# Triangle attention and triangle multiplication: four-bank sums, a new run-out, and all constants added by TensorE

## The chip, the cores and the metric

The kernel runs on one core of a Trainium2 chip. The metric is the device time of one execution in microseconds, the median of several runs; for the kernel before it is 250.66 us (three runs, 250.49 to 250.67).

## The reference

`x` is a map of 96 x 96 tokens with 32 channels. Two residual layers follow each other, each on a group norm `_gn` of its input with one channel to a group (mean and variance over all 9216 tokens).

```python
x = x + L0(_gn(x));  x = x + L1(_gn(x))
# L0: triangle attention, 4 heads of 32, one softmax row per (i, q, head)
xn = layernorm(x) * ln_gamma + ln_beta
scores = einsum('biqhd,biKhd->bihqK', q, k) + tri_bias + mask_bias
o = einsum('bihqk,bikhd->biqhd', softmax(scores), v) * sigmoid(xn @ wg + bg)
out = o @ wo + bo
# L1: triangle multiplication
zn = layernorm(z) * ln_in_w + ln_in_b
a = mask * sigmoid(zn @ a_g + ..) * (zn @ a_p + ..);  b likewise
t = einsum('bikh,bjkh->bijh', a, b)
out = sigmoid(zn @ g_w + g_b) * ((layernorm(t) * ln_out_w + ln_out_b) @ z_w + z_b)
```

All of it is float32.

## The kernel before, in words

Rows of the map are taken in 24 blocks of four rows, and six quads of four blocks. Every engine has its own program, and semaphores tie them; the order of each engine's work is written out by hand, and each engine works its list off in that order. PSUM has eight banks of 512 float32 columns, which the stages share.

**Attention loop.** 72 tiles of 128 queries, in 36 pairs. `step_pe`, `step_act`, `step_dve`, `step_pool` write out step k of each engine, 40 steps in all. ScalarE takes the exponentials of pair k (`exponentials`, L763); VectorE inverts the sums (L1119); GpSimd multiplies pair k-1 by them (L572); TensorE turns pair k-2 into banks 2 and 3 (L1418); VectorE copies both banks (L1131); TensorE multiplies pair k-3 with the values into bank 1 (L1432). A finished block g of four rows is gated by VectorE (`o_group`, L1140), projected by TensorE (`y_group`, L1443) into the same bank 1, and added to the residual (L1145), which releases `y_added`. The run-out is steps 35 to 39, in which no new pair comes in. In it TensorE also turns residual quads 0 to 3 (`res_transposes`, L1220), which ScalarE copies (`res_copy`, L646).

**Second norm** (`norm_front(1)`). VectorE sums what `y_added` released, ScalarE takes squares of the last blocks (L778), a matmul spreads the statistic (L1240), residual quads 4 and 5 are turned behind it, and 24 matmuls center the quads (L1263; two records each). ScalarE squares them (L680), VectorE sums the squares over channels (L964) in two parts of three quads, ScalarE takes the root (L697), VectorE scales (L973), TensorE turns the normalized quads (L1291) and ScalarE copies them (L702). `idle_products` are matmuls whose result nobody reads; the list `IDLE` says how many stand at each place.

**Projection loop.** Eight sets of three blocks: TensorE projects (L1473, L1478), VectorE multiplies one part by the mask (L1165), ScalarE takes sigmoids (L834 for a and b, L836 for the output gate), VectorE multiplies (L1175). GpSimd meanwhile prepares quads 0 and 1: gate times z constant, added to the residual (L616, L618, `CONST_SETS`).

**Tail.** 32 products per channel fill all eight banks (L1497). VectorE subtracts a pivot into SBUF (L1045), ScalarE squares (L842), GpSimd adds squares (L598). VectorE adds the eight banks up (`add_scores`, L1034, L1032; each releases its bank through `sums_read`), makes the variance, and ScalarE the root (L849). TensorE turns the maps (L1523), multiplies by the z weights (`z_products`, L1508), and for quads 2 to 5 adds the z constant times the deviation (`z_constant`, L1515). Quads 0 and 1 are gated by VectorE before the root (L1014), scaled by ScalarE in 32 pieces (L858), and added to the residual by GpSimd (L456). Quads 2 to 5 have their gates scaled first (L450, by VectorE for quad 2, by GpSimd for 3 to 5), and then VectorE gates and adds. The twelve stores (L436) go out in three batches of two quads each: `FIRST`, `SECOND`, `EARLY`, issued from the queues of SP and ScalarE, each behind a wait for `out_ready` or `out_more`.

## Time and profile before

| | |
|---|---|
| median of three runs | 250.66 us |
| the profiled execution, its own time | 250.1 us |
| its span, first to last instruction | 248.3 us |
| mean granted TensorE clock | 0.969 |
| TensorE busy | 213.9 us (86%) |
| VectorE busy | 184.7 us (74%) |
| ScalarE busy | 188.2 us (76%) |
| GpSimd busy | 110.1 us (44%) |
| output stores | 12 of 96.0 KB, eight issued by SP, four by ScalarE |

The span is shorter than the execution's own time by 1.8 us, which lie ahead of the first and behind the last instruction. Engines are named as in the page of the profile: PE is TensorE (PEld its weight loads), DVE VectorE, ACT ScalarE, POOL GpSimd, SP the queue of SyncE. A float32 matmul may leave two records. A timeline row gives the start and the length of a piece, and in brackets how long the engine stood before it and what ended that.

### The profile page before, as it was taken

How to read it: one execution, taken by the hardware profiler on the slowest of the kernel's cores; microseconds unless marked ns; L12 is line 12 of the kernel's file. 1: busy time of each engine (PE TensorE's matmuls, PEld its weight loads, DVE VectorE, ACT ScalarE, POOL GpSimd, SP SyncE). 2: the span in 40 equal slices, each digit the busy share in tenths (PEclk: the TensorE clock that was granted, in tenths of full speed). 3: DMA queues.
4: the chain of work that ended last, by engine and by line, in shares of the span. 5: the costliest groups of instructions: out<-in, count | busy, mean ns of one | idle time of the engine just before them, and what ended most of it. 6: DMA issues, size and time to landing. Idle time of an engine off the chain costs nothing. (4 is left out here: it accounts for less than half of the span.)

```text
span 248.3 us, 6918 instructions
## 1 busy us (share of the span) xinstructions
PE 213.9 (86%) x2492; PEld 184.7 (74%) x2492; DVE 184.7 (74%) x356; ACT 188.2 (76%) x792; POOL 110.1 (44%) x110
## 2 busy tenths in 40 slices
PE   6979984789999999999999999999879875697830
PEld 6969733678889889888888889888758764596510
DVE  6755867446878787787888797787658859979890
ACT  0765982799988999899989989999855865676380
POOL 2100001067575765857675675844500328036281
PEclk9997999799999999999999999999999999999985
DMA  8500035665454646454464644330000000000038
GB/s 128 90 13 15 8 127 168 238 238 181 166 199 151 243 150 215 154 194 167 164 226 141 235 162 154 130 134 3 0 3 3 0 3 0 4 0 3 0 65 127
DMA packets 42992, 27.30 MB, mean 110 GB/s; under 512 B 24976, under 2 KB 42942, under 8 KB 42958
## 3 DMA queue, kind: packets, MB, share of 16 engines
q1 hardware_dynamic: 38614, 26.27, 33.1%
q10 hardware_dynamic: 4216, 0.51, 1.5%
q8 instruction: 20, 0.33, 0.5%
q0 software_dynamic: 128, 0.08, 0.2%
q14 instruction: 14, 0.11, 0.1%
HBM read 1.36 MB, written 1.18 MB: 10 GB/s over the span
## 5 line engine op out<-in xcount | busy, mean ns | idle before, releaser
L763 ACT ACTIVATE maps<-psum,neg_max 128x96 f32<-128x96 f32 x288 | 94.8, 356 | 10.5 <-PE psum L1418 7.2
L572 POOL TENSOR_TENSOR maps<-maps,rden 128x768 f32<-128x768 f32 x36 | 53.0, 1472 | 43.9 <-DVE rden L1119 43.9
L763 ACT ACTIVATION_READ_ACCUMULATOR maps<-psum,neg_max 128x1 f32 x288 | 63.8, 221 | 0.0
L1109 DVE TENSOR_REDUCE neg_max<-psum 128x8 f32<-128x768 f32 x36 | 34.5, 958 | 28.4 <-PE psum L1392 28.4
L1131 DVE COPY turned<-psum 96x1024 f32<-96x1024 f32 x36 | 43.6, 1212 | 5.2 <-PE psum L1418 3.8
L1418 PE MATMUL psum<-ident,maps 128*96 128x128 f32 x288 | 37.5, 273 | 1.6 <-DVE turned L1131 0.8
L1418 PEld LDWEIGHTS psum<-ident,maps 128*96 128x96 f32 x288 | 31.6, 126 | 3.1 <-DVE turned L1131 1.1
L1385 PE MATMUL psum<-u_st,x_stack 128*128 128x384 f32 x72 | 25.7, 358 | 2.1 <-DMA u_st<-u_split 2.1
L1191 PE MATMUL psum<-tri_b,ones_r 128*96 128x192 f32 x187 | 23.0, 278 | 2.6 <-DVE ones_r L888 2.2
L1387 PE MATMUL psum<-u_st,x_stack 128*96 128x384 f32 x72 | 24.8, 345 | 0.0
L1392 PE MATMUL psum<-bias_lo,token_ident 100*128 100x384 f32 x72 | 24.8, 344 | 0.0
L1390 PE MATMUL psum<-bias_hi,token_ident 96*128 96x384 f32 x72 | 24.8, 344 | 0.0
L1432 PE MATMUL psum<-turned,maps 128*32 128x96 f32 x768 | 23.3, 250 | 1.1 <-DVE shared L1145 1.1
L1191 PEld LDWEIGHTS psum<-tri_b,ones_r 128*96 128x96 f32 x187 | 20.4, 182 | 3.5 <-DVE ones_r L888 2.2
L581 POOL TENSOR_TENSOR u_split<-u_full,u_split 128x384 fp32r<-128x384 f32 x21 | 21.2, 1008 | 1.7
L1432 PEld LDWEIGHTS psum<-turned,maps 128*32 128x32 f32 x768 | 15.6, 109 | 7.7 <-issue 6.4
L806 ACT ACTIVATE g_sb<-psum,bg_half 128x384 f32<-128x384 f32 x24 | 14.4, 600 | 2.9 <-PE psum L1364 2.9
L1385 PEld LDWEIGHTS psum<-u_st,x_stack 128*128 128x128 f32 x72 | 13.9, 193 | 2.5 <-issue 2.5
L579 POOL CAST u_split<-u_full 128x384 fp32r<-128x384 f32 x21 | 10.6, 506 | 11.4 <-DVE u_full L1125 11.4
L1390 PEld LDWEIGHTS psum<-bias_hi,token_ident 96*128 96x128 f32 x72 | 13.8, 192 | 1.2
L772 ACT ACTIVATE maps<-psum 96x512 f32<-96x512 f32 x24 | 14.4, 602 | 0.0
L1374 PEld LDWEIGHTS psum<-wv_st,x_stack 128*96 128x96 f32 x96 | 10.9, 164 | 4.7 <-DVE u_full L1125 4.2
(199 smaller groups left out, 417.5 us busy)
## 6 DMA issues: line engine op xcount, KB each, us to landing
u_st<-u_split SPq DMA_DIRECT2D x96, 192.0 KB
x_stack<-shared SPq DMA_DIRECT2D x40, 96.0 KB, 2.0
maps<-in_x SPq DMA_DIRECT2D x8, 144.0 KB, 3.5
out_y<-maps SPq DMA_DIRECT2D x8, 96.0 KB, 2.3
x_stack<-shared SPq DMA_DIRECT2D x4, 144.0 KB, 2.1
bias_lo<-gate_sb SPq DMA_DIRECT2D x24, 18.0 KB
out_y<-maps ACTq DMA_DIRECT2D x4, 96.0 KB, 3.7
x_stack<-shared SPq DMA_DIRECT2D x4, 48.0 KB, 1.9
```

The lines of the kernel that those rows point to most:

```text
L572: pool.tensor_tensor(at, at, rden[:, rows, :].unsqueeze(3).to_broadcast([P, 2, H, N]), ALU.mult).then_inc(probs_ready, 1)
L581: pool.tensor_tensor(u_split[:, g % U_SLOTS, 1], u_full[:, :], u_split[:, g % U_SLOTS, 0].bitcast(f32), ALU.subtract).then_inc(u_lo, 1)
L763: e = act.activation(probs[:, t // 2 % SLOTS, t % 2, h], bank_s[t % 4][:, h * N:(h + 1) * N], ACT.Exp, bias=neg_max[:, t % BODY, h:h + 1], ...
L1109: dve.tensor_reduce(neg_max[:, rows_of(k), :], scores.rearrange("p r (h k) -> p r h k", h=H), AX.X, ALU.max, negate=True).then_inc(max_rea ...
L1131: dve.tensor_copy(turned[0:N, :, 2 * (j % SPAN):2 * (j % SPAN) + 2].rearrange("p h n t -> p n h t"), psum[0:N, 2 * BANK:4 * BANK].rearrang ...
L1191: pe.matmul(banks[bank][0:N, 0:PW + C], ones_r[:, :], tri_b[:, 0:PW + C], start=True, stop=True)
L1385: pe.matmul(bank_s[t % 4][:, 0:H * N], x_columns[:, last - N:last + P - N], u_st[:, g % STAGES, :, GROUP - 1, :], start=True, stop=False)
L1387: pe.matmul(bank_s[t % 4][0:N, 0:H * N], x_stack[:, i, g, :], u_st[:, g % STAGES, :, i, :], start=True, stop=False, skip_group_check=True)
L1390: pe.matmul(scores, token_ident[0:N, i], bias_hi[0:N].rearrange("p h k -> p (h k)"), start=False, stop=False)
L1392: pe.matmul(scores, token_ident[0:MASK_ROWS, i], bias_lo[0:MASK_ROWS, g % STAGES, i].rearrange("p h k -> p (h k)"), start=False, stop=True ...
L1418: mm = pe.transpose(bank_t[n][0:N, h * P:(h + 1) * P], probs[:, j % SLOTS, n, h, :], ident[:, :])
L1432: mm = pe.matmul(bank_o[h * C:(h + 1) * C, i * N:(i + 1) * N], values[:, g % V_SLOTS, i, h * C:(h + 1) * C], probs_t, start=True, stop=True)
```

## The change

Four places are touched.

- *Run-out.* GpSimd multiplies only the first tile of the last pair, VectorE the second. The last pair is turned into banks 4 and 5 instead of 2 and 3, in the same step as the pair before it. The last block's output goes to bank 3 instead of bank 1. The last gate is projected one step earlier. Residual quads 0 to 2 (instead of 0 to 3) are turned in steps 37 and 38, and ScalarE copies them after the loop; 3 to 5 follow behind the statistic matmul. Six idle products before the last projection go.
- *Second norm.* For the last three quads GpSimd adds the two halves of the 32 squares first, and VectorE sums 16. Ten idle products become two.
- *Projection loop.* GpSimd's preparation of quads 0 and 1 goes; TensorE adds the constants of all six quads.
- *Tail.* The sums over eight banks become two reductions over four banks each. GpSimd adds all the squares and folds them. No quad is gated ahead of the root. The gates of quad 0 are scaled by VectorE, of 1 to 3 by GpSimd, of 4 and 5 by ScalarE in 32 pieces; GpSimd adds the residual of quads 1 and 3, VectorE of the others. The stores go out in the order of the quads.

```diff
--- before.py
+++ after.py
@@ constants @@
-POOL_QUADS = 2
-FIRST, SECOND, EARLY = (2, 3), (4, 5), (0, 1)
+POOL_SCALES, ACT_SCALES, POOL_ADDS = (1, 2, 3), (4, 5), (1, 3)
...
 def gate_group(k):
+            if k >= PAIRS:
+                return BLOCKS - 1 if k == PAIRS else None
...
-        RES_EARLY = 4
-        RES_BANKS = 4
+        RES_EARLY = 3
         def res_bank(q):
-            return 4 + q % RES_BANKS
+            return (6, 7, 4, 5, 7, 4)[q]
+        def turning_bank(j):
+            return 4 if j == PAIRS - 1 else 2
+        def turned_at(k):
+            if k >= PAIRS:
+                return (PAIRS - 2, PAIRS - 1) if k == PAIRS else ()
+            return (k - T_BEHIND,) if live(k - T_BEHIND) else ()
+        def out_bank(g):
+            return banks[3] if g == BLOCKS - 1 else bank_o
...
-        IDLE = (32, 6, 8, 4, 2, 3, 6, 10, 24)
+        IDLE = (32, 6, 8, 4, 2, 3, 6, 2, 24)
@@ sync: the stores @@
-            for quads, rows in ((FIRST, range(GROUP)), (SECOND, range(2)), (EARLY, range(2))):
-                if quads[0]:
-                    sp.wait_ge(out_ready, quads[-1] + 1 - POOL_QUADS)
-                else:
-                    sp.wait_ge(out_more, POOL_QUADS)
+            for quads, rows, ready, more in (((0, 1), range(GROUP), 1, 1), ((2, 3), range(2), 2, 2), ((4, 5), range(2), 4, 2)):
+                sp.wait_ge(out_ready, ready)
+                sp.wait_ge(out_more, more)
@@ gpsimd @@
                 if live(k - 1):
+                    tiles = 1 if k == PAIRS else 2
+                    at = probs[:, (k - 1) % SLOTS, 0:tiles]
...
+            for q in parts(1)[1]:
+                at = slice(4 * q, 4 * q + 4)
+                pool.wait_ge(d_squared, QUADS + q + 1)
+                pool.tensor_tensor(work[:, at, :, 0:C // 2], work[:, at, :, 0:C // 2], work[:, at, :, C // 2:C],
+                                   ALU.add).then_inc(d_folded, 1)
...
-                for n in range(1, TRI_BANKS - 1):
+                for n in range(1, TRI_BANKS):
...
+                pool.wait_ge(squares_added, TRI_BANKS - 1)
+                pool.tensor_tensor(square_parts[:, :, 0:2], square_parts[:, :, 0:2], square_parts[:, :, 2:4],
+                                   ALU.add).then_inc(squares_added, 1)
+                pool.wait_ge(squares_added, TRI_BANKS)
+                pool.tensor_tensor(moments[:, 2], square_parts[:, :, 0], square_parts[:, :, 1],
+                                   ALU.add).then_inc(squares_added, 1)
...
-                for q in range(POOL_QUADS + 1, QUADS):
+                for q in POOL_SCALES:
                     scale_gates(pool, q).then_inc(gates_scaled, 1)
-                for q in range(POOL_QUADS):
-                    pool.wait_ge(scaled_more, q + 1)
+                for n, q in enumerate(POOL_ADDS):
+                    pool.wait_ge(z_gated, n + 1)
                     add_residual(pool, q).then_inc(out_more, 1)
-            for n in range(CONST_SETS):
...
-                pool.wait_ge(gates_ready, 2 * n + 2)
-                pool.tensor_tensor(product, gate_sb[:, at], constant, ALU.mult).then_inc(const_gated, 1)
-                pool.tensor_tensor(res[:, at], res[:, at], product, ALU.add).then_inc(const_gated, 1)
@@ scalar @@
-                for q in (2 * (k - PAIRS), 2 * (k - PAIRS) + 1):
-                    if 0 <= q < RES_EARLY:
-                        res_copy(q)
...
             load_table(2, ACT.Sqrt)
+            res_copy(0)
+            res_copy(1)
             square_outputs(QUADS - 1, slice(BLOCKS - 4, BLOCKS - 1))
             square_outputs(QUADS, slice(BLOCKS - 1, BLOCKS))
+            res_copy(2)
...
-            for q in range(POOL_QUADS):
-                act.wait_ge(z_gated, q + 1)
+            for q in ACT_SCALES:
                 for b in range(4 * q, 4 * q + 4):
                     for f in range(GROUP):
-                        scaled = act.activation(square[:, b, f], square[:, b, f], ACT.Copy, scale=inverse[:, b, f:f + 1])
+                        scaled = act.activation(gate_sb[:, b, f], gate_sb[:, b, f], ACT.Copy, scale=inverse[:, b, f:f + 1])
...
@@ vector @@
+                        if layer and part:
+                            dve.wait_ge(d_folded, q + 1 - QUADS // 2)
+                            members_of = slice(0, C // 2)
...
+                        ins = dve.tensor_reduce(tok[:, 0, at], work[:, at, :, members_of], AX.X, ALU.add)
...
+                def total_of(n):
+                    four = psum[0:N, 4 * n * BANK:4 * (n + 1) * BANK].rearrange("j (k x) -> j k x", k=4)[:, :, 0:GN]
+                    dve.tensor_reduce(halves[:, n], four.rearrange("j k (h f b) -> j b f k h", h=GROUP, f=GROUP), AX.XY,
+                                      ALU.add).then_inc(sums_read, 1)
...
-                for n in range(TRI_BANKS):
-                    add_scores(n)
+                for n in range(2):
+                    total_of(n)
...
-                for q in range(POOL_QUADS):
-                    gate_z(q).then_inc(z_gated, 1)
                 dve.wait_ge(root_ready, 6)
...
+                if k == PAIRS - 1:
+                    dve.wait_ge(exp_done, TILES - 1)
+                    dve.reciprocal(rden[:, last.start, :], den[:, last.start, :]).then_inc(rden_ready, 1)
...
+                if k == PAIRS - 1:
+                    dve.wait_ge(exp_done, TILES)
+                    dve.reciprocal(rden[:, last.stop - 1, :], den[:, last.stop - 1, :]).then_inc(rden_ready, 1)
+                    at = probs[:, (PAIRS - 1) % SLOTS, 1]
+                    dve.wait_ge(rden_ready, PAIRS + 1)
+                    dve.tensor_tensor(at, at, rden[:, last.stop - 1, :].unsqueeze(2).to_broadcast([P, H, N]),
+                                      ALU.mult).then_inc(last_scaled, 1)
...
-                if y is not None:
+                if y is not None and g != BLOCKS - 1:
                     dve.wait_ge(y_done, y + 1)
...
-            link(scale_gates(dve, POOL_QUADS))
-            for q in range(POOL_QUADS, QUADS):
-                need(dve, gates_scaled, q - POOL_QUADS)
-                link(gate_z(q))
-                add_residual(dve, q).then_inc(out_ready, 1)
+            link(scale_gates(dve, 0))
+            for q in range(QUADS):
+                if q in POOL_SCALES:
+                    dve.wait_ge(gates_scaled, POOL_SCALES.index(q) + 1)
+                elif q in ACT_SCALES:
+                    dve.wait_ge(scaled_more, ACT_SCALES.index(q) + 1)
+                if q in POOL_ADDS:
+                    gate_z(q).then_inc(z_gated, 1)
+                else:
+                    link(gate_z(q))
+                    add_residual(dve, q).then_inc(out_ready, 1)
@@ tensor @@
+                for j in turned_at(k):
...
+                        pe.wait_ge(exp_done, TILES)
+                        pe.wait_ge(probs_ready, PAIRS)
+                        pe.wait_ge(last_scaled, 1)
...
+                if k == PAIRS + 1:
+                    res_transposes(0)
...
-                        idle_products(IDLE_BANKS[0], IDLE[6])
...
+                if PAIRS < k < STEPS - 1:
+                    res_transposes(k - PAIRS)
...
-                    pe.wait_ge(sums_read, GROUP + q + 1)
+                    pe.wait_ge(sums_read, 2)
...
-                if q < GROUP:
-                    pe.wait_ge(sums_read, q + 1)
+                if not q:
+                    pe.wait_ge(sums_read, 1)
...
-            for q in (2, 3, 4):
+            for q in range(5):
                 z_constant(q)
```

## Rows read from the trace of the kernel before

**Rows 1.** Chain of waits, in order of time: start, length (us), what.

```profile
185.42 0.34 DVE shared L1145 x2
...
198.68 1.07 PE psum L1191 x10
...
224.66 0.48 DVE turned L1034
```

**Rows 2.** Timeline of GpSimd, run-out: start, length (us), line, operation, [idle before].

```profile
174.78 1.47 POOL L572 TENSOR_TENSOR maps<-maps,rden 128x768 f32<-128x768 f32 x1 [0.69 <-DVE rden L1119]
177.53 1.47 POOL L572 TENSOR_TENSOR maps<-maps,rden 128x768 f32<-128x768 f32 x1 [1.28 <-DVE rden L1119]
```

**Rows 3.** Timeline of TensorE, run-out.

```profile
179.78 1.08 PE L1418 MATMUL psum<-ident,maps 128*96 128x128 f32 x8 [0.85 <-DVE turned L1131]
```

**Rows 4.** Timeline of VectorE, run-out.

```profile
175.42 1.22 DVE L1131 COPY turned<-psum 96x1024 f32<-96x1024 f32 x1 [0.72 <-PE psum L1418]
...
180.90 1.22 DVE L1131 COPY turned<-psum 96x1024 f32<-96x1024 f32 x1 [1.17 <-PE psum L1418]
```

**Rows 5.** Timeline of TensorE, second norm.

```profile
186.80 1.05 PE L1220 MATMUL psum<-ident,shared 128*96 128x128 f32 x8
...
188.39 5.48 PE L1263 MATMUL psum<-centering_r,shared 128*96 128x128 f32 x48 [0.18 <-DVE centering_r L952]
```

**Rows 6.** Windows, projection loop: stretch, its length, busy us by engine, clock, DMA.

```profile
203.00:218.40 15.40, 10.37 (x208) 8.31 (x201) 14.67 (x15) 9.26 (x16) 6.95 (x6) 1.00 0.01 3
```

**Rows 7.** Line L1175, durations ns min/median/max.

```profile
L1175 DVE TENSOR_TENSOR shared<-maps,turned x6: 942/1058/1664, 204.5 to 217.3; 96x768 f32<-96x768 f32 x6
```

**Rows 8.** Timeline of all engines, start of the projection loop.

```profile
204.33 0.99 POOL L618 TENSOR_TENSOR res_memory<-res_memory,u_split 96x384 f32<-96x384 f32 x1
204.47 1.66 DVE L1175 TENSOR_TENSOR shared<-maps,turned 96x768 f32<-96x768 f32 x1
```

**Rows 9.** Timeline of ScalarE, second norm.

```profile
195.27 1.99 ACT L702 ACTIVATE shared<-psum,w_all 128x384 f32<-128x384 f32 x3
197.52 0.24 ACT L697 ACTIVATE tok<-tok 96x48 f32<-96x48 f32 x1 [0.27 <-DVE tok L981]
```

**Rows 10.** Lines L1109 and L992, the reductions: durations ns min/median/max.

```profile
L1109 DVE TENSOR_REDUCE neg_max<-psum x36: 957/958/959, 45.7 to 171.5; 128x8 f32<-128x768 f32 x36
...
L992 DVE TENSOR_REDUCE u_split<-ident x1: 249/249/249, 190.4 to 190.4; 96x32 f32<-96x96 f32 x1
```

**Rows 11.** Timeline of TensorE, tail.

```profile
225.27 2.87 PE L1523 MATMUL psum<-ident,maps 96*128 96x96 f32 x24 [1.20 <-DVE turned L1034]
227.98 3.66 PE L1508 MATMUL psum<-g_sb,shared 128*96 128x128 f32 x32
...
233.72 1.95 PE L1515 MATMUL psum<-u_split 32*96 32x512 f32 x6
```

**Rows 12.** Timelines of GpSimd and ScalarE, tail.

```profile
222.50 5.57 POOL L598 TENSOR_TENSOR turned<-turned,maps 96x384 f32<-96x384 f32 x5
...
241.12 1.75 POOL L456 TENSOR_TENSOR maps<-maps,res_memory 96x512 f32<-96x512 f32 x1 [1.24 <-ACT maps L858]
...
234.15 6.89 ACT L858 ACTIVATE maps<-maps,tok 96x32 f32<-96x32 f32 x32 [0.95 <-DVE tok L1063]
```

**Rows 13.** Timeline of VectorE, tail.

```profile
235.28 0.69 DVE L1014 TENSOR_TENSOR maps<-psum,gate_sb 96x512 f32<-96x512 f32 x1 [0.44 <-DVE gate_sb L450]
236.00 1.30 DVE L456 TENSOR_TENSOR maps<-maps,res_memory 96x512 f32<-96x512 f32 x1
...
241.06 0.69 DVE L456 TENSOR_TENSOR maps<-maps,res_memory 96x512 f32<-96x512 f32 x1
```

**Rows 14.** Windows, stores: DMA share and GB/s are the last two columns.

```profile
244.00:246.00 2.00, 0.00 (x0) 0.00 (x0) 0.00 (x0) 0.00 (x0) 0.00 (x0) 0.50 1.30 189
```

**Rows 15.** Windows, first norm: the granted clock is the third column from the end.

```profile
14.00:16.00 2.00, 1.05 (x8) 0.84 (x8) 0.68 (x1) 1.57 (x2) 0.00 (x0) 1.00 0.01 1
...
18.00:20.00 2.00, 2.00 (x11) 2.00 (x10) 0.87 (x2) 0.59 (x1) 0.00 (x0) 0.50 0.08 20
```

111 lines of the change are left out of this document (49 added, 62 removed).

## The prediction

> **What bounds the kernel now.** First the chain of waits read in order of time [rows 1]: TensorE, VectorE and ScalarE hand one thread to each other, and no engine is the limit everywhere. So each stretch the diff touches is read in its timelines, for the wait that ends last there.
>
> *Run-out of the attention loop, to 185.76 us.* GpSimd normalizes the last pair of tiles from 177.53 to 179.00 [rows 2]; TensorE turns it only at 179.78, having waited for VectorE to copy the pair before out of the same two banks [rows 3]; VectorE copies it at 180.90 [rows 4], and the run-out ends with the last residual add at 185.76 [rows 1].
>
> *Second norm, 185.8 to 203.6.* Behind the statistic matmul stand the transposes of two residual quads; on the chain then 5.48 us of centering [rows 5], and later ten idle products, 1.07 us, ahead of the fourth group of transposes [rows 1].
>
> *Projection loop, 203.6 to 218.3.* VectorE is busy 14.67 of 15.40 us, GpSimd 6.95 [rows 6]. One of VectorE's products lasts 1.66 us, the quickest of that line 0.94 [rows 7].
>
> *Tail, 218.4 to 248.3.* VectorE adds eight banks one by one, TensorE makes the z products, root and gates follow, and the twelve stores end it.
>
> **The change part by part.** Times are on the clock of the profiled run before (span 248.3 us, 250.1 us in all, so 1.8 around it; 0.56 below the median 250.66). The sum is taken off the median.
>
> *Run-out.* The pair 34 leaves GpSimd at 174.78 + 1.47 = 176.25 [rows 2]. Of pair 35 GpSimd now takes the first tile only, 384 elements, about 1.0 us by a 384-element row (0.99, [rows 8]): to 177.27. VectorE takes the second, after copying pair 33 (175.4 + 1.2 = 176.6, some 0.2 earlier without the residual transposes ahead of it [rows 4]) and a short reciprocal. This product reads two tensors from SBUF, as GpSimd's does. Such a meeting is in [rows 8]: VectorE's product starts at 204.47 while GpSimd runs until 205.32 and takes 1.66, which is 0.85 of waiting and 0.81 of work; so VectorE stands until 177.27 and ends near 177.8.
>
> The Trainium skill, "SBUF — State Buffer", section "Who interferes with whom", makes a rule of it: VectorE with two SBUF inputs and GpSimd exclude each other for a whole instruction, while VectorE with one SBUF input is free. The trace agrees in the waiting of 0.85 us above; by sharing in place of waiting the run-out would gain some 0.4 more.
>
> TensorE turns pair 35 at 177.9 into banks 4 and 5, with no wait for VectorE (179.78 before). VectorE's queue then decides: output 21 and residual 20 (0.75), the copy of 34 to 179.75, the copy of 35 to 180.9, against 180.90 + 1.22 = 182.12: 1.2 us. The rest of the gain is order: the last value products write bank 3, so they wait for output 22 alone (181.4), not for the residual add behind it; the last output is formed ahead of residual 22; six idle products go. Chain: 181.4, value products 0.9, output 0.5, y 0.4, add 0.45: 183.7. Gain 2.05. Costed at nothing: the new wait for the last exponentials, with output 21 queued behind it on VectorE, since ScalarE is done with them before the copy of 33 ends at 176.6; the last gate's projection, a step earlier behind a wait for output 21, since only residual quad 0 queues behind it; ScalarE's table load and two residual copies ahead of the squares, done by 182.4, where the squares can start at 183.0. Uncovered, each would cost its own half to one us once. But a third residual quad now stands behind the statistic matmul: four more transposes at 0.81/8 each are 0.41, of which 0.18 us of TensorE's idle time ahead of centering hides a part [rows 5]. **Term: -1.8** (bounds -2.5 with sharing and a hidden quad, -1.0 if the order gains nothing).
>
> *Second norm.* GpSimd halves the squares of three quads (96x256 each; 0.7 to 1.4 us by its products of 0.99 for 384 elements, slowed or not [rows 8]) and has been idle there, so VectorE's three sums of 512 become 256, saving 3 x 256 x 1.04 ns = 0.8 us. But ScalarE is busy with three copies from 195.27 to 197.26 and takes the root at 197.52 [rows 9], so only 0.25 reaches the root. The idle products 10 to 2 are worth more: eight of the ten in 1.07 us are 0.86, and 0.78 by their starts, as the norm that it needs ends near 198.7, 0.25 earlier, and it can start at 198.8 instead of 199.6. ScalarE's table load ends near 199.0, in time for the transposed quad at 199.3. The two gains overlap; the second contains the first. **Term: -0.8** (bounds -0.3 with slow folds, -1.0).
>
> *Projection loop.* GpSimd's six products for the constants go. VectorE's slowest product falls from 1.66 to about 1.0 (the line's median is 1.06 [rows 7]), 0.65; I put the others that meet GpSimd, some above the median, at 0.45 together. VectorE has no gap in the loop, and ScalarE and TensorE have, so nothing else is late at once. **Term: -1.1** (-0.6 to -1.4).
>
> *Tail, sums.* Copy and seven adds of one bank each become two reductions of 1536 elements. No row shows one over two axes of four banks. A contiguous one of 768 from PSUM takes 0.958 us, a strided one of 96 takes 0.25 [rows 10]: both about 1.04 ns an element. I take that: 1.75 us each, from 224.66, where the copy starts [rows 1], to 228.2. Bounds: half as much, or 4 ns an element. VectorE's thread gets shorter; TensorE's longer: its transposes need the first bank only, at 225.27, and now the first reduction, 226.5. Hence 24 transposes (2.71 to the next group) to 229.3 and 32 z products (3.66) to 232.9 [rows 11]. Before, they ended at 231.64 and the constants came 2.08 us later, of which the turned root and eight z products fill 1.1; so TensorE had 1.0 us of waiting for the root there, which is now used up. GpSimd adds the eighth square and folds twice: 228.07 [rows 12] + 1.1 + 0.5 + 0.4 and gaps, 230.5, with VectorE's small sums locked between them; root inverted by 232.4 against 234.1 (ScalarE's scalings start there, [rows 12]). That 1.7 us is not passed on: the gates need the z constants, which start at 233.9 against 233.72 [rows 11], so the first gate stays near 235.3, as before [rows 13].
>
> *Tail, gates.* From 235.3 VectorE has six gates (0.66) and four adds (0.69, up to 1.30 beside GpSimd [rows 13]) in place of four and four. ScalarE's 32 scalings start at 233.4 behind the turned root and last 6.9: 240.3 [rows 12], before the sixth gate needs them. Constants at 0.65 (1.95 for three) finish five by 237.2 and the sixth near 239.4, in time. With the lock, the adds of GpSimd end at 238.8 and 241.3, VectorE's last at 243.3. Stores: quads 2 and 3 leave at 241.3 (before: a second batch at 241.75, behind VectorE's last add [rows 13]), the last four at 243.3 (before 242.87, behind GpSimd's [rows 12]). The eight last stores of 96 KB at 189 GB/s [rows 14] take 4.2 us, so the earlier batch sets the end; the first batch's four issues on SP's queue run from 238.8 and are through before it. **Term: -0.4** (-1.3 if constants and adds run free, +1.0 if the last batch sets the end).
>
> Sum: -1.8 - 0.8 - 1.1 - 0.4 = -4.1: 250.66 - 4.1 = **246.6 us** (246.0 in a profiled run like this).
>
> **Rivals.**
> *TensorE's clock falls in the tail.* It was granted 1.2 GHz in 18 to 20 us after idling for half of 14 to 16 [rows 15]. The change widens its gap before the transposes from 1.2 to 2.4 us. For: the gap doubles. Against: the clock stayed at full speed through the projection loop, where it is idle for a third [rows 6]. Price: the two microseconds at half speed in that row lose 1.0, a spell half as long again 1.5 to 1.7: up to 248.3. The Trainium skill, "TensorE: Matmul & The Clock Gate", section "HAM oscillation — how this bites in real kernels", tells of such falls behind waits.
>
> *The run-out passes on little*, because VectorE's queue meets GpSimd a second time or ScalarE is late: half its term, 247.5.
>
> *The tail gives more:* the constants start earlier than I think or the adds meet no lock, -1.3: 245.7.
>
> *Slower: the wide reductions.* If strides over four banks cost 4.2 ns an element (four times the row's 1.04), the two end at 237.8, the z products start there instead of 229.3, and 8.5 us are added: 255. It decides from 2.9 ns an element, where it eats all 4.1 us. For it: no row has that shape. Against: both reduction rows, strided or not, go at 1.04.
>
> *The change does not do what it says:* the folds come late and the idle products were needed; 0.4 lost, inside the range.
>
> **How the numbers follow.** Forecast 0.60, own range 245.5 to 247.8 (the terms' bounds, half of each way together). Clock 0.13, run-out 0.10, tail better 0.10, slow reductions 0.05, anything else 0.02. The range 245.0 to 248.6 leaves out the slow reductions and the far ends. A measurement here can tell 0.2%, 0.5 us, from no change. Faster 0.91, same 0.03, slower 0.06, the last from the reductions with a little of the rest.
>
> **What would show it.** Right: last residual add near 183.7; TensorE's wait of 0.85 gone; VectorE's products in the projection loop all under 1.1; two reductions of about 1.75; first gate about 17 us after the first score matmul, as now. Wrong: reductions over 3 us; a granted clock of 0.5 between the scores and the constants; a second-half sum waiting for GpSimd beyond 0.5 us; VectorE idle between projection products.

## The result, and the profile after

The changed kernel takes 247.87 us (median of four executions, 245.44 to 248.35) against 250.66 us on the same chip (250.49 to 250.81): a ratio of 0.987, 95% interval 0.982 to 0.992. That is 2.8 us less, where 4.1 were forecast, and inside the range. Measured again beside the first experiments it took 246.6 us against 251.5, a ratio of 0.980 (0.977 to 0.983). Its executions scatter by 3 to 4 us, more than its distance from the forecast. Much of what follows is about that. In the table of the experiments the 95% intervals leave out two executions (249.76 us of after_again, 252.65 us of tail) that stood over 1.5% above the fastest of their kernel.

The profiled execution took 247.51 us and has a span of 245.7 us, 2.6 under the 248.3 of before. The chain of waits, in order of time (start, length, what):

```profile
206.50 1.58 PE psum L1511 x24
208.60 1.53 PE psum L1511 x24
...
216.74 5.66 PE psum L1530 x64
222.98 1.67 DVE turned L1044
224.79 2.17 PE psum L1556 x24
```

Against [rows 1] two things stand out. The two reductions that replace the copy and the adds put VectorE on the chain only until the first of them ends; TensorE carries the chain from there. And two groups of the projection, 24 matmuls each, are on the chain at 1.58 and 1.53 us; in the loop of before VectorE bounded, and such a group took 0.98 to 1.01 us in its timeline.

To say where the 2.6 us come from, the span is cut at four events that every kernel here has: the start of the last accumulation read of the attention's exponentials (ScalarE), the first centering product of the second norm, the first score matmul, the end. From the timelines:

| | start to last read | to centering | to scores | to the end |
|---|---|---|---|---|
| before | 175.64 | 12.75 | 30.03 | 29.88 |
| after | 176.76 | 10.93 | 29.05 | 28.96 |

So run-out -1.82, norm and loop -0.98, tail -0.92: -3.72. Code that the change does not touch took 1.12 longer, which leaves -2.6. Most of that 1.12 is there when the first norm's centering ends, at 25.04 us in place of 24.21. Windows of after (length, busy us of TensorE, its weight loads, VectorE, ScalarE and GpSimd, granted clock, DMA share, GB/s), to be read with [rows 15]:

```profile
14.00:16.00 2.00, 1.05 (x6) 0.86 (x6) 0.61 (x1) 1.49 (x2) 0.00 (x0) 0.81 0.03 9
18.00:20.00 2.00, 2.00 (x11) 2.00 (x11) 0.59 (x4) 0.59 (x1) 0.00 (x0) 0.50 0.07 18
...
207.00:208.00 1.00, 1.00 (x23) 0.74 (x17) 0.56 (x1) 0.83 (x2) 0.00 (x0) 0.50 0.00 0
```

TensorE is at 1.2 GHz from about 15.3 to 22.1 us here, and from about 17.9 to 21.3 before, by windows of one us. The last row is from the second finding: a stretch at 1.2 GHz from 206 to 210 us, inside the projection loop, where [rows 6] has 1.00 throughout.

**Run-out.** Its timeline (start, length, line, operation, [idle before]):

```profile
175.90 2.25 POOL L587 TENSOR_TENSOR maps<-maps,rden 128x768 f32<-128x768 f32 x2 [0.69 <-DVE rden L1124]
...
177.71 2.05 PE L1441 MATMUL psum<-ident,maps 128*96 128x128 f32 x16
...
177.78 0.79 DVE L1144 TENSOR_TENSOR maps<-maps,rden 128x384 f32<-128x384 f32 x1
...
184.61 0.32 DVE L1159 SCALAR_TENSOR_TENSOR shared<-psum,bo_col,res_memory 128x96 f32<-128x96 f32 x1 [0.34 <-PE psum L1472]
```

TensorE turns both last pairs in one piece of 2.05 us, without the wait of [rows 3]. The last residual add ends at 184.95, or 183.83 without the 1.12; 183.7 was forecast.

**Second norm, timeline.** The sums of the last three quads are now 256 wide, but the root of ScalarE still stands behind its copies, as in [rows 9]. The short operation between the sums and the root (195.72) took 0.72 us, against 0.18 for the same operation on the first three quads (191.84) and in the kernel before; it ended at 196.44, 0.05 behind a GpSimd product that was running (194.48):

```profile
192.05 2.48 POOL L606 TENSOR_TENSOR maps<-maps 96x256 f32<-96x256 f32 x3 [13.89 <-ACT maps L697]
...
194.47 1.99 ACT L719 ACTIVATE shared<-psum,w_all 128x384 f32<-128x384 f32 x3
...
194.48 1.91 POOL L611 TENSOR_TENSOR u_split<-u_split,g_sb 96x1024 f32<-96x1024 f32 x1
...
194.62 1.06 DVE L983 TENSOR_REDUCE tok<-maps 96x16 f32<-96x256 f32 x3
...
195.72 0.72 DVE L1000 TENSOR_SCALAR tok<-tok 96x48 f32<-96x48 f32 x1
196.47 0.24 ACT L714 ACTIVATE tok<-tok 96x48 f32<-96x48 f32 x1
```

**Projection loop, timeline.** The lines of products (durations min/median/max), to be read with [rows 7], then where VectorE stood:

```profile
L1189 DVE TENSOR_TENSOR shared<-maps,turned x6: 944/950/1070, 203.0 to 215.6; 96x768 f32<-96x768 f32 x6
```

```profile
206.34 1.74 PE L1511 MATMUL psum<-w_all,shared 32*96 32x160 f32 x24
...
208.15 0.95 DVE L1179 TENSOR_TENSOR maps<-psum,mask_t 96x768 f32<-96x768 f32 x1 [0.59 <-PE psum L1511]
208.40 1.68 PE L1511 MATMUL psum<-w_all,shared 32*96 32x160 f32 x24
...
210.16 0.95 DVE L1179 TENSOR_TENSOR o_sb<-psum,mask_t 96x768 f32<-96x768 f32 x1 [0.19 <-PE psum L1511]
```

The product of 1.66 us is gone. But VectorE, which before did not wait in the loop once it had begun at 203.6, waits for the two slow groups.

**Tail.** Timeline, to be read with [rows 11] and [rows 13]:

```profile
221.89 5.57 POOL L619 TENSOR_TENSOR turned<-turned,maps 96x384 f32<-96x384 f32 x5
...
222.90 3.41 DVE L1044 TENSOR_REDUCE turned<-psum 96x96 f32<-96x1536 f32 x2
...
224.79 2.17 PE L1556 MATMUL psum<-ident,maps 96*128 96x96 f32 x24 [2.40 <-DVE turned L1044]
...
226.34 0.26 DVE L1057 TENSOR_TENSOR turned<-turned 96x96 f32<-96x96 f32 x1
226.63 0.94 DVE L1058 SCALAR_TENSOR_TENSOR turned<-turned 96x96 f32<-96x96 f32 x1
...
226.80 3.66 PE L1541 MATMUL psum<-g_sb,shared 128*96 128x128 f32 x32
...
228.69 0.26 DVE L1061 TENSOR_TENSOR turned<-turned 96x96 f32<-96x96 f32 x1 [0.45 <-POOL turned L625]
...
231.35 1.97 PE L1548 MATMUL psum<-u_split 32*96 32x512 f32 x10
...
232.55 0.69 DVE L1030 TENSOR_TENSOR maps<-psum,gate_sb 96x512 f32<-96x512 f32 x1 [1.55 <-PE psum L1548]
```

A reduction takes 1.74 us, as forecast. TensorE waits 2.40 us for the first (1.20 for the copy before); then its transpositions, z products and constants follow one another without a gap. The first gate comes 15.81 us behind the first score matmul (16.86 before), although VectorE now stands for 1.55 us ahead of it.

### The profile page after: what moved, and what is told of

It is laid out like the page before. It is cut to its first block, busy times and chain, and to the rows that moved or that the text cites. A ratio compares the mean times of both kernels' runs of the same rounds, so it can differ in the third digit from the quotient of the medians.

```text
span 245.7 us, 6891 instructions
## 1 busy us (share of the span) xinstructions
PE 213.8 (87%) x2482; PEld 184.9 (75%) x2482; DVE 183.6 (75%) x348; ACT 187.8 (76%) x792; POOL 105.2 (43%) x110
## 4 chain that ended last, share of the span: by engine, by line
PE 65%; DVE 12%; ACT 7%; issue 7%; DMA 3%; SPq 2%; POOL 1%; DVEq 0%; ACTq 0%
PE psum L1441 9%; PE psum L1461 6%; PE psum L1288 5%; PE psum L1410 5%; PE psum L1417 5%; PE psum L1412 5%; PE psum L1415 5%; PE psum L1399 4%; PE psum L1389 3%; PE psum L1530 2%; DVE neg_max L1110 2%; SPq L482 2%; DVE shared L1189 2%; PE psum L1511 2%; DVE u_full L1130 2%
## 5 line engine op out<-in xcount | busy, mean ns | idle before, releaser
L587 POOL TENSOR_TENSOR maps<-maps,rden 128x768 f32<-128x768 f32 (+1 forms) x36 | 52.3, 1454 | 42.4 <-DVE rden L1120 41.7
L1211 PE MATMUL psum<-tri_b,ones_r 128*96 128x192 f32 x173 | 20.7, 272 | 2.6 <-DVE ones_r L902 2.2
L596 POOL TENSOR_TENSOR u_split<-u_full,u_split 128x384 fp32r<-128x384 f32 x21 | 21.2, 1009 | 1.7
L1211 PEld LDWEIGHTS psum<-tri_b,ones_r 128*96 128x96 f32 x173 | 18.2, 176 | 3.3 <-DVE ones_r L902 2.2
```

Of the source, the lines that this page charges most:

```text
L587: pool.tensor_tensor(at, at, rden[:, rows, :].unsqueeze(3).to_broadcast([P, tiles, H, N]), ALU.mult).then_inc(probs_ready, 1)
L596: pool.tensor_tensor(u_split[:, g % U_SLOTS, 1], u_full[:, :], u_split[:, g % U_SLOTS, 0].bitcast(f32), ALU.subtract).then_inc(u_lo, 1)
L1211: pe.matmul(banks[bank][0:N, 0:PW + C], ones_r[:, :], tri_b[:, 0:PW + C], start=True, stop=True)
```

## The experiments

Twelve kernels were measured in three groups of four, each group beside its own runs of before (medians 251.5, 250.7 and 250.4 us); times of different groups are best compared by their ratios to before. One execution of each was profiled; it is one of those that its median is taken over, and not always a typical one. The ranges hold every execution. The table has the same four stretches, and where the granted clock was below 2.4 GHz between the second norm and the last constant, in whole us.

| kernel | to last read | to centering | to scores | to the end | 1.2 GHz | median (range), us | ratio to before, 95% |
|---|---|---|---|---|---|---|---|
| after_again | 175.93 | 10.92 | 29.01 | 28.74 | 205-209 | 246.60 (245.57-249.76) | 0.977-0.983 |
| idle_ten | 176.62 | 10.93 | 28.86 | 31.19 | 223-231 | 247.83 (246.18-249.41) | 0.981-0.990 |
| warm_start | 176.33 | 10.99 | 28.14 | 29.94 | 223-228 | 247.86 (247.21-249.54) | 0.983-0.990 |
| no_constants | 177.51 | 12.76 | 28.95 | 29.88 | 227-231 | 249.93 (249.33-250.89) | 0.992-0.997 |
| keep_clock | 175.78 | 10.93 | 28.86 | 28.83 | none | 246.54 (246.07-248.15) | 0.981-0.988 |
| tail | 176.09 | 12.75 | 28.96 | 31.20 | 225-232 | 249.53 (248.43-252.65) | 0.992-0.998 |
| runout | 175.40 | 10.92 | 29.93 | 29.85 | 224-228 | 248.27 (247.81-249.35) | 0.987-0.993 |
| norm | 176.67 | 12.75 | 30.05 | 29.83 | 202-207 | 249.70 (249.12-251.12) | 0.994-0.998 |
| eight_adds | 175.51 | 10.94 | 29.07 | 28.58 | 205-209 | 246.00 (244.60-247.10) | 0.976-0.984 |
| same_rows | 175.06 | 10.94 | 28.97 | 30.23 | 199-203, 223-227 | 247.58 (246.27-249.23) | 0.983-0.991 |
| pair_on_pool | 175.21 | 11.67 | 29.13 | 31.59 | 200-204, 223-231 | 247.36 (246.08-249.39) | 0.982-0.991 |
| early_and_warm | 175.29 | 10.93 | 29.11 | 28.97 | 204-209 | 245.41 (245.03-246.10) | 0.975-0.983 |

### The kernel again, and its idle products

**after_again** is the kernel after, unedited.

> The changed kernel once more, nothing edited. Clock theory: its time is spread by stretches that TensorE was granted 1.2 GHz for; in the profiled run such a stretch lay at 15.4 to 22.3 us in the first norm (before: 18.0 to 21.2) and one at 206.3 to 209.6 us in the projection loop (before: none). Then the times of the runs go with their mean granted clock: about 245.5 us at a clock of 0.968, 247.5 to 248.4 at 0.949 to 0.956, and a run without the second stretch and with the short first one is some 5 us under the kernel before. Rival: the spread comes from DMA or elsewhere; then time and mean clock do not go together.

Measured: 246.6 us, and a profile like the first, with the stretch in the loop at 205 to 209 us. The times go roughly with the mean granted clock, as the theory has it: 245.57 and 245.76 us at 0.969 and 0.970, 246.75 at 0.956, 249.76 at 0.946, with 247.22 at 0.966 out of line.

**idle_ten**

```diff
-        IDLE = (32, 6, 8, 4, 2, 3, 6, 2, 24)
+        IDLE = (32, 6, 8, 4, 2, 3, 6, 10, 24)
```

> The changed kernel with ten idle products ahead of the fourth transposed quad, as before the change, in place of two. If the two idle products were what lets the clock fall in the projection loop, the fall between 203 and 212 us is gone in every run, the spread is smaller, and the median is lower than the changed kernel's by up to 0.5 us although 0.8 us of idle products is back on the path. Rival: the idle products have nothing to do with it, the removal is worth its 0.8 us: this kernel is 0.7 to 0.8 us slower than the changed one at the same clock, and falls of the clock come as often.

Measured: no stretch in the loop, and yet 247.83 us. The stretch came later, in the tail. Windows over the loop and over the start of the tail, then TensorE's timeline in the tail:

```profile
202.00:216.00 14.00, 10.18 (x212) 8.28 (x204) 13.34 (x15) 8.93 (x16) 0.00 (x0) 1.00 0.01 3
223.00:231.00 8.00, 6.54 (x39) 6.57 (x40) 6.71 (x9) 3.32 (x8) 5.58 (x7) 0.57 0.01 2
```

```profile
224.46 4.07 PE L1556 MATMUL psum<-ident,maps 96*128 96x96 f32 x24 [2.40 <-DVE turned L1044]
228.33 4.73 PE L1541 MATMUL psum<-g_sb,shared 128*96 128x128 f32 x32
```

Transpositions 4.07 us in place of 2.17, z products 4.73 in place of 3.66: the first rival of the prediction, TensorE's clock falling in the tail. So the theory holds for the stretch in the loop, in this one profile, and misses on the times: the median is 1.2 us above that of after_again, and the scatter, 3.2 us, is no smaller.

**warm_start**: idle products in the gaps of the start.

```diff
-        IDLE_FIRST = (12, 3, 24, 22, 8, 20, 4)
+        IDLE_FIRST = (12, 6, 24, 44, 8, 20, 4)
...
                     first_weights()
+                    idle_products(IDLE_BANKS[0], 10)
...
             u_projection(0)
+            idle_products(6, 10)
...
             u_projection(1)
+            idle_products(6, 10)
```

> The changed kernel with idle products in the idle gaps of TensorE in the first norm (ten ahead of the second statistic, three more behind it) and while it waits for the first staged operand (ten behind each of the first two projections, 44 in place of 22). Clock theory: the stretches at 1.2 GHz at 15 to 22 and 45 to 49 us go or shorten, the first scores start 1 to 3 us earlier, the run-to-run spread shrinks to under 1 us, and the median falls to 244 to 246 us. Rival: those stretches are hidden behind transfers or do not depend on the idle gaps: median within 0.5 us of the changed kernel's, same spread.

Measured: the stretch of the first norm is gone, and VectorE's first maximum of the scores comes at 44.23 us, against 47.10 in after. But the last read comes at 176.33 us, no earlier than elsewhere (175.06 to 177.51): TensorE then waits for a staged operand, and a stretch that lay at 46 to 49 us in after lies at 49 to 53 here. The median, forecast at 244 to 246 us, is 247.86. TensorE's timeline:

```profile
46.80 0.44 PE L1411 MATMUL psum<-u_st,x_stack 128*128 128x384 f32 x1 [1.90 <-DMA u_st<-u_split]
```

It is the one profile with two idle products in the second norm and no stretch in the loop. There centering to scores is 28.14 us, 1.89 under before: the -0.8 and -1.1 of the prediction. Its tail had a stretch of its own and took 29.94.

**no_constants**: the kernel before without GpSimd's constants.

```diff
-        CONST_SETS = -(-4 * POOL_QUADS // TRIO)
+        CONST_SETS = 0
```

> The kernel before, with GpSimd's six products and sums for the constants of quads 0 and 1 left out (their output lacks the z constant). It prices what that work costs VectorE in the projection loop. Lock theory (GpSimd and VectorE exclude each other when both read two operands from SBUF): VectorE's slowest product of the loop falls from 1.66 us to 1.05 or less, the loop from 14.7 to 13.6 us, the kernel from 250.66 to 249.6 us, if no fall of the clock comes in the loop. Rival: those products are slow for another reason, or TensorE and ScalarE take over as the bound: loop 14.4 us or more, kernel within 0.4 us of before.

Measured: centering to scores 28.95 against 30.03 us, 1.08 less, both at 2.4 GHz. The loop's term stands by itself. The median is 1.6 under before (by the interval 0.8 to 2.1).

### Each part alone, and a filler for the tail

**keep_clock** is idle_ten with ten products of constant operands, into PSUM partitions that nobody uses, while VectorE makes the first reduction.

```diff
             pe.wait_ge(deviated, TRI_BANKS)
+            for _ in range(10):
+                pe.matmul(banks[7][N:P, 0:N], ones_r[:, 0:C].bitcast(f32), tri_b[:, 0:N].bitcast(f32), start=True, stop=True)
```

> The kernel after with the second norm's idle products back at 10, as in idle_ten, and with ten more products of 96 columns on TensorE, of constant operands into unused PSUM partitions, put between the scores and the first transposition, so that TensorE works while VectorE makes the first four-bank reduction. Theory: the 1.2 GHz stretch that idle_ten's tail showed (223.8 to 230.7; transpositions 4.07 us, z products 4.52) came because TensorE stood for 2.4 us behind the scores. Then the transpositions take 2.2 us, the z products 3.5, the clock is 1.00 from the scores to the last constant, and scores to end is 28.7 to 29.2 us against 31.2 in idle_ten: a median of 245.5 to 246.5, 1.5 to 2 us under idle_ten. Rival: the stretch comes at its own time whatever TensorE does just then: transpositions or z products again near 4 us, scores to end above 30, a median of 247.5 or more.

Measured: 246.54 us, just above the theory's range, and in the profile the tail is at 2.4 GHz. A window from the scores to the last constant, and TensorE's timeline:

```profile
215.57:235.00 19.43, 18.03 (x169) 15.29 (x169) 15.16 (x23) 13.04 (x44) 12.54 (x13) 1.00 0.00 1
```

```profile
221.86 1.84 PE L1536 MATMUL psum<-tri_b,ones_r 128*32 128x96 f32 x20 [0.65 <-DVE maps L1051]
223.63 2.20 PE L1558 MATMUL psum<-ident,maps 96*128 96x96 f32 x24
225.67 3.66 PE L1543 MATMUL psum<-g_sb,shared 128*96 128x128 f32 x32
```

Scores to end is 28.83 us against 31.19 in idle_ten; only the filler differs. The rival, a stretch that comes at its own time, was to end above 30, which this profile does not show. The times do not settle it: against their own runs of before, keep_clock is at 0.984 and idle_ten at 0.985, and the five executions of keep_clock that were not profiled had mean clocks of 0.953 to 0.967, all below the 0.974 of the profiled one.

**tail**, **runout** and **norm** are the kernel before with one part of the diff each. Their hunks are those of the change: for tail the constants, sums, scales and stores; for runout the last pair, its banks and the residuals; for norm the folds and `IDLE[7]` from 10 to 2.

> The kernel before with the projection loop's and the tail's hunks alone (no constants on GpSimd ahead of the root, four-bank sums, PE's constants for all six quads, ACT's scales, stores in three groups); run-out and second norm as before. Theory: centering to scores goes from 30.0 to 28.95 us, as in no_constants, if the loop keeps 2.4 GHz, and scores to end from 29.9 to 28.8 us if the tail keeps it: 2.1 us in all, 248.4 against 250.5. With a 1.2 GHz stretch in the tail scores to end is 29.9 to 31.2, and the time 249.5 to 250.8. Rival: the tail's gain needs the other hunks (the earlier arrival): scores to end above 29.6 with the clock at 1.00.

Measured: 28.96 us from centering to scores, and 31.20 to the end with a stretch at 225 to 232, in an execution of 250.89 us, 1.4 above this kernel's median. The median is 1.2 under before, where 2.1 was forecast at 2.4 GHz. No profile shows these hunks alone with the tail at 2.4 GHz, so the rival, that the tail's gain needs the other hunks, is not settled by this run.

> The kernel before with the run-out's hunks alone (last pair scaled by two engines, its turning and residuals rearranged); everything from the second centering on as before. Theory: from the start of the last exponential's accumulation read to the second centering 10.9 us instead of 12.75, that is 1.8 us less, and nothing of it lost behind: centering to scores 30.0 (at 2.4 GHz), scores to end 29.9, the median 1.6 to 2.0 us under before. Rival: run-out passes on little, since the second norm's first reductions find the stage before them no earlier: under 1.0 us.

Measured: 10.92 us to the centering, 1.83 less, nothing lost behind it; median 2.4 under before, by the interval 1.7 to 3.2 (1.6 to 2.0 forecast). This profile also had a stretch in its tail, with the old sums, and lost nothing by it (29.85 against 29.88). A window and TensorE's timeline say why:

```profile
224.00:228.00 4.00, 3.97 (x26) 3.83 (x25) 3.73 (x9) 2.60 (x6) 1.74 (x2) 0.57 0.01 4
```

```profile
223.10 3.90 PE L1566 MATMUL psum<-ident,maps 96*128 96x96 f32 x24 [1.20 <-DVE turned L1051]
226.79 4.06 PE L1551 MATMUL psum<-g_sb,shared 128*96 128x128 f32 x32
230.69 0.25 PE L1572 MATMUL psum<-ident,tok 96*96 96x96 f32 x1
```

The slow transpositions and products end just as the root is ready. In the kernel before TensorE waits 0.99 us at that place, the spare time that the prediction found and called used up:

```profile
232.63 0.29 PE L1529 MATMUL psum<-ident,tok 96*96 96x96 f32 x1 [0.99 <-ACT tok L849]
```

no_constants shows the same: a stretch at 227 to 231, and 29.88.

> The kernel before with the second norm's hunks alone (GpSimd folds the last three quads' squares to half width, the reductions read half, idle products 10 to 2); run-out, loop and tail as before. Theory: the run-out is unchanged (12.75 us from the last accumulation read to the centering), centering to scores 29.2 instead of 30.0 us at 2.4 GHz, scores to end 29.9: 0.8 us under before. Rival: the fewer idle products let the clock fall in the projection loop: 1.2 GHz for some 3 us between the second norm and the scores, products of the projection at 1.7 us instead of 1.0, centering to scores at 30.0 or more and no gain.

Measured: median 1.0 under before (by the interval 0.6 to 1.6), but the profiled execution, the slowest of its twelve with 251.12 us, shows the rival. A window of the loop, then TensorE's timeline:

```profile
203.00:204.00 1.00, 1.00 (x22) 1.00 (x17) 0.00 (x0) 0.48 (x2) 0.44 (x1) 0.50 0.00 0
```

```profile
202.56 0.59 PE L1485 MATMUL psum<-tri_b,ones_r 32*96 32x480 f32 x4 [0.85 <-ACT shared L709]
...
202.87 1.86 PE L1490 MATMUL psum<-w_all,shared 32*96 32x160 f32 x23
```

The second set's projection (202.56) starts 13.14 us behind the centering (202.56 - 189.42) against 13.86 before (202.25 - 188.39), so 0.72 were won; the stretch then took them all: 30.05 to the scores.

### The sums, the constants, the last pair, the stores

**eight_adds** is the kernel after with the copy and the seven adds of one bank in place of the two reductions.

```diff
-                for n in range(2):
-                    total_of(n)
-                dve.wait_ge(sums_read, 2)
+                for n in range(TRI_BANKS):
+                    add_scores(n)
+                dve.wait_ge(sums_read, TRI_BANKS)
```

> The kernel after with the four-bank reductions replaced by the copy and seven bank adds of the kernel before (TensorE's transpositions of a bank wait for that bank's add again); constants, scales and stores as after. Theory: the four-bank sums give most of the tail's gain and also expose TensorE: with the adds, scores to end is 29.6 to 30.0 us at 2.4 GHz instead of 28.8, and a 1.2 GHz stretch in it costs under 0.3, since an add of some 0.56 us paces each four transpositions; scores to first gate is 16.5 to 17.0 us against 15.8; the median 0.5 to 1.0 us above the 246.6 to 247.9 of the kernel after, and less scattered. Rival: the tail's gain comes from the constants and the order of the stores: scores to end stays at 28.7 to 29.1.

Measured: 28.58 us from scores to end, and 246.0 in the median. By this profile the theory, that the four-bank sums give the tail its gain, is wrong. Timeline of this kernel's tail:

```profile
222.26 4.05 DVE L1045 TENSOR_TENSOR turned<-turned,psum 96x384 f32<-96x384 f32 x7
...
222.37 2.87 PE L1559 MATMUL psum<-ident,maps 96*128 96x96 f32 x24 [1.20 <-DVE turned L1047]
225.08 3.66 PE L1544 MATMUL psum<-g_sb,shared 128*96 128x128 f32 x32
228.93 0.29 PE L1565 MATMUL psum<-ident,tok 96*96 96x96 f32 x1 [0.20 <-ACT tok L866]
...
231.23 0.69 DVE L1030 TENSOR_TENSOR maps<-psum,gate_sb 96x512 f32<-96x512 f32 x1 [0.84 <-PE psum L1551]
```

TensorE begins 1.2 us sooner behind the scores and is slowed by the adds, so the z products start 9.56 us behind the first score matmul (225.08 - 215.52), against 10.06 with reductions (226.80 - 216.74). The first gate comes at 15.71 us against 15.81. The reductions save VectorE 1.2 us (copy and adds 0.54 + 4.05, reductions 3.41), on an engine that waits for constants anyway. The tail's gain is therefore in the rest. What the timelines suggest, and no run takes by itself, is the root: VectorE's three sums of squares no longer stand ahead of it, nor its two early gates (1.28 us, 232.18 in the kernel before) ahead of its inverse, and TensorE waits 0.20 us for it here, against 0.99 before. In after the first gate already comes 1.05 us earlier than before, and the end 0.92.

**same_rows**: all constants from rows 0 to 31.

```diff
                 rows = slice(32 * (q // 2), 32 * (q // 2) + 32)
+                rows = slice(0, 32)
```

> The kernel after with all six quads' constants read from rows 0 to 31 of both operands (the constants of quads 2 to 5 are thereby those of other channels). Theory: the five constants ahead of quad 5 took 1.97 us, as three did before (1.95), because constants in different groups of 32 rows run side by side; two of one group in a row make four passes. In one group ten passes follow one another at 0.43 us: 4.4 to 4.6 us for the ten. The time does not change by more than 0.4 us, since VectorE needs a constant only every 1.2 us or more. Rival: they run one after the other anyway: 1.97 again.

Measured, in TensorE's timeline:

```profile
231.23 4.53 PE L1549 MATMUL psum<-u_split 32*96 32x512 f32 x10
```

4.53 us against 1.97: operands in different groups of 32 rows do run side by side. The Trainium skill, "TensorEngine Tiling (Array Packing)", section "Tiling Modes", says under its key properties that different tiles can execute weight loads and matmuls in parallel; the trace agrees. From the start of the constants to the end it is 13.97 us (245.2 - 231.23) against 14.35 in after (245.7 - 231.35), so the 2.6 us cost nothing. The longer tail (30.23) is the stretch at 223 to 227, ahead of the constants.

**pair_on_pool**: GpSimd scales both tiles of the last pair.

```diff
-                    tiles = 1 if k == PAIRS else 2
+                    tiles = 2
...
-                    dve.tensor_tensor(at, at, rden[:, last.stop - 1, :].unsqueeze(2).to_broadcast([P, H, N]),
-                                      ALU.mult).then_inc(last_scaled, 1)
```

> The kernel after with the last pair's second tile scaled by GpSimd again, in one instruction for the whole pair, and not by VectorE; all else of the run-out as after. Theory: TensorE's last eight transpositions then begin when GpSimd ends near 2.5 us behind the start of the last accumulation read, about 0.4 us later than now: from that start to the second centering 11.2 to 11.6 us (after 10.92, before 12.75), so the split is worth 0.3 to 0.7 us and the new order of turning and residuals the rest of the 1.8. Rival: the split is what gives the run-out's gain: 12.3 us or more.

Measured: 11.67 us to the centering, 0.75 more than after and 1.08 less than before, a little over the theory's range. So two engines on the last pair are worth 0.75 and the new order the other 1.08. The rows in the timeline:

```profile
176.30 1.47 POOL L587 TENSOR_TENSOR maps<-maps,rden 128x768 f32<-128x768 f32 x1 [0.48 <-DVE rden L1138]
...
177.91 1.05 PE L1433 MATMUL psum<-ident,maps 128*96 128x128 f32 x8 [0.67 <-POOL maps L587]
```

**early_and_warm** is the kernel after with keep_clock's ten products and with earlier stores.

```diff
-            for quads, rows, ready, more in (((0, 1), range(GROUP), 1, 1), ((2, 3), range(2), 2, 2), ((4, 5), range(2), 4, 2)):
+            for quads, rows, ready, more in (((0,), range(GROUP), 1, 0), ((1,), range(GROUP), 1, 1), ((4, 5), range(3), 4, 2)):
...
-            for quads, ready in (((2, 3), 2), ((4, 5), 4)):
+            for quads, rows, ready in (((2, 3), range(GROUP), 2), ((4, 5), range(3, GROUP), 4)):
```

> The kernel after with the ten idle products behind the scores as in keep_clock (idle products of the second norm left at 2), and with stores sent earlier: SyncE stores quad 0 as soon as it is added, then quad 1, then three of four row groups of quads 4 and 5; ScalarE stores quads 2 and 3 and the last row group. Theory: the tail keeps 2.4 GHz in every execution and the stores begin about 1.2 us earlier, so that fewer bytes are left behind the last add: scores to end 27.5 to 28.4 us against 28.83 in keep_clock, a median of 245.0 to 246.0. Rival: the last add and what follows it set the end, whatever was stored before: scores to end 28.7 to 29.0, 246.5.

Measured: 245.41 us, the lowest median of all, and the narrowest range, of four executions. But not by the stores: scores to end is 28.97 us against 28.83 in keep_clock. Windows:

```profile
235.00:239.00 4.00, 0.00 (x0) 0.00 (x0) 3.93 (x6) 1.24 (x6) 1.26 (x2) 0.54 0.60 98
239.00:243.00 4.00, 0.00 (x0) 0.00 (x0) 0.36 (x1) 0.00 (x0) 0.00 (x0) 0.50 1.11 174
```

While SyncE alone issues the early stores of 48 KB, the DMA engines are busy for 0.60 of the time and move 98 GB/s; later, with both queues, 174 (180 in after from 239 to 244). From the end of the last add to the end of the span it is 4.9 us in both kernels (244.3 - 239.36 and 245.7 - 240.76). Whether this version beats the kernel after is not settled: its interval against before, 0.975 to 0.983, meets that of after_again.

## Why the prediction came out as it did

**Run-out, -1.8: right.** -1.82 in the profile of after, -1.83 with this part alone, nothing lost behind it, 0.75 of it by the two engines.

**Second norm, -0.8: lost in most profiles, kept in the medians.** The gain is there: 0.72 in norm, and 1.89 together with the loop in warm_start. The weak step is the sentence "The idle products 10 to 2 are worth more: eight of the ten in 1.07 us are 0.86", which prices them as cost only. In the profiles they go with TensorE's clock in the loop. In the six profiles with ten of them (before, idle_ten, keep_clock, no_constants, tail, runout) the clock is 1.00 in the loop; in seven of the eight with two there is a stretch at 1.2 GHz between 199 and 210 us. idle_ten is the single edit behind that count, with one profile. Such a stretch gives back 0.7 to 1.0 us (28.97 to 29.13 against 28.14; 0.72 in norm). With ten products centering to scores is 28.86, so in the profiles the edit won 0.7 without the stretch and lost 0.1 to 0.3 with it. The prediction named this ("the idle products were needed; 0.4 lost") among the rivals with no chance of its own to speak of. The executions that were not profiled say otherwise: norm's median is 1.0 under before, and idle_ten's 1.2 above that of after_again in the same group, so over all executions the term was not lost. How often the stretch comes in them is open.

**Projection loop, -1.1: right.** -1.08 in no_constants; no product above 1.07 us.

**Tail, -0.4: mis-sized, both ways.** At 2.4 GHz it is -0.9 to -1.1 (28.74 to 28.96), and the first gate came 15.81 us behind the scores, not "about 17 us" as before. TensorE began its transpositions 8.05 us behind the scores (8.08 forecast), but they took 2.0 us and not 2.71: the 2.71 of [rows 11] was the pace of VectorE's adds, not TensorE's own. Five constants took 1.97 and not 3.25: the three in [rows 11] cost 1.95 because two of them share a group of rows, and so do four of the five here, in two groups side by side. The sums gain nothing, as the prediction had it ("not passed on"), and against adds they lose 0.2 to 0.4.

**The clock in the tail, a rival at 0.13: it comes often, by another way, and dearer.** Of the seven profiles with four-bank sums and no filler, five have a stretch between the scores and the constants. They end 29.94 to 31.59 us behind the first score matmul, 1.1 to 2.8 more than keep_clock; 1.7 was forecast at most. The reason given, that the gap grows from 1.2 to 2.4 us, is at most half of it: runout and no_constants had a stretch with the gap of 1.20. What the change did was to use up the 0.99 us for which TensorE waited there, so a slow stretch now moves the end. In keep_clock, with a filler in the gap, there is no stretch; that is one profile, and its cause is argued, not shown. A rival is in the table: whether the tail has a stretch also goes with the loop. Without a filler, the four profiles with a stretch that began after 202 us in the loop (after, after_again, norm, eight_adds) have none in the tail, and of the eight others all but before have one. So the ten idle products may move a stretch into the tail, where it costs more, rather than remove it. early_and_warm had its stretch in the loop, and so does not tell whether its filler did anything. The Trainium skill, "TensorE: Matmul & The Clock Gate", section "HAM oscillation — how this bites in real kernels", traces such falls to waits for DMA. In this the trace differs: here the waits are for other engines, 2.40 us the longest between the scores and the constants.

**The sum.** Without stretches the parts are 10.93, 28.14 and 28.83 us, each seen in some profile though not all in one: 4.8 under before (72.66), against 4.1 forecast. With them an execution loses 0.7 to 1.0 in the loop, 1.1 to 2.8 in the tail, or both. What comes ahead of the run-out, which the change leaves alone, adds its own scatter: the last read comes at 175.06 to 177.51 us over fourteen profiles. That is how a kernel forecast at 246.6 measured 247.87 once and 246.6 the second time. That second figure hits the forecast in part by luck: before measured 251.5 beside it, so the change was worth 4.9 us there and 2.8 the first time, with the forecast 4.1 between them. The medians of three parts alone (runout, norm, tail), 2.4, 1.0 and 1.2 under before, add up to 4.6. The prediction's "own range", 245.5 to 247.8, is not what its bounds give: half of each way is -1.05 and +1.6, so 245.5 to 248.2, and 247.87 lies between the two upper ends.

**The Trainium skill's rule of the lock** ("SBUF — State Buffer", "Who interferes with whom"), on which the loop and the small sums rest: VectorE's sum of two SBUF operands at 226.63 took 0.94 us, its neighbour of the same width 0.26, and ended at 227.57, 0.1 behind the last of the GpSimd adds that ran from 221.89 (to 227.46). The trace agrees. The prediction's short form, that VectorE with one SBUF input is free, goes too far: the section makes an exception for VectorE's two-port modes, and the operation at 195.72, with one SBUF input, took 0.72 us beside GpSimd in place of 0.18. All eight profiles with the folds show 0.72 or 0.73 there, the six others 0.18. It cost nothing, since the root waited for ScalarE's copies to 196.46 anyway.

**The other rivals.** The run-out passed on all. The wide reductions took 1.14 ns an element (1.744 us for 1536), far from 2.9. The prediction's "about 1.04 ns an element" is not what [rows 10] give as they stand (958 ns for 768 elements are 1.25 each, 249 for 96 are 2.6); it needs a fixed part of some 0.15 us taken off each row, an estimate from the two of them, and with it 1536 elements come to 1.75. Of the second norm's second-half sums none waited for GpSimd: its folds ended at 194.53, the first sum started at 194.62. In the tail a sum waited 0.45 us for GpSimd (228.69).

## What to carry to other kernels

Products that compute nothing may be holding the clock of what comes later: before one takes them out, read the granted clock of the stages that follow, in more than one profile, and the medians beside them. When spare time of TensorE ahead of a wait is used up, price what a stretch at 1.2 GHz would then cost, because it was free until then. A row whose pace another engine sets is no price for the same work after that engine is gone.

## What the runs showed of the hardware

- Matmuls of 32 rows on different row groups ran side by side: ten took 1.97 us over three groups, 4.53 in one.
- With the same code, stretches at 1.2 GHz came at different places in different profiles: in the first norm at 15.3 to 22.1 us in after, at 17.8 to 21.2 in after_again. With the loop free of one, the tail had one (idle_ten); with the first norm free of one, the stretch at 46 to 49 us came at 49 to 53 (warm_start).
- Output stores of 48 KB issued by one queue moved 98 GB/s with the DMA engines busy for 0.60 of the time, stores from two queues at the end 174 to 180 GB/s; an earlier start of the stores gained nothing in the one profile that has it.
- A VectorE operation with a single SBUF input of 48 elements took 0.72 us beside a running GpSimd product and 0.18 without one.
